# Attention scores as two rounded products over 128 stacked rows, and y and values in paired calls, in a decoder layer on one core

## The chip, the cores and the metric

One Trainium2 chip, one of its cores. The metric is the device time of one execution of the whole kernel in microseconds (us). TensorE (PE, with PEld for its weight loads), VectorE (DVE), ScalarE (ACT) and GpSimd (POOL) each run a list of instructions of their own in order and wait for each other by semaphores; SyncE (SP) issues the DMAs.

## The reference

A decoder layer over 64 sequences of 256 tokens and 256 features: a state-space mixer, cross attention of the 256 tokens to 376 rows (120 of a context, 256 of the sequence itself), and a gated "twist" block with three cycles. Each block is added to its input and normalised. The part that the change touches first is the attention, 8 heads of 64 features:

```python
q = ln @ Wq
kv = jnp.concatenate([xn, ln], axis=-2) @ Wkv
k, v = jnp.split(kv, 2, axis=-1)
q, k, v = (to_heads(q) * scale, to_heads(k), to_heads(v))
sim = jnp.einsum('bhid,bhjd->bhij', q, k)
attn = jax.nn.softmax(sim, axis=-1)
out = jnp.einsum('bhij,bhjd->bhid', attn, v)
```

The other part is the product of a chunk of the mixer, `y`, of the decay matrix `Lm` (tokens by tokens, per head) with `xdt` (tokens by 64 features, per head).

## The kernel before

The kernel is written by hand as one list of calls for each engine, and these lists set the order; there is no scheduler. A call such as `scores(s, c, i)` belongs to sequence `s`, and each engine has its own function of that name or of the step that follows it. In the steady loop (`for p in range(2, NSEQ - 1)`) three sequences are in work at once: `m` in the mixer, `a = m - 1` in the attention, `f = m - 2` in the twist block. Each pass of the loop finishes one sequence of work on each engine.

A result of TensorE goes to one of 8 PSUM banks. The scores take banks 1 to 3 in turn, the attention's other products 4 and 5, the mixer's 6 and 7, and the twist block bank 0. A bank is taken again when the engine that reads it has signalled.

Three kinds of TensorE product occur. Most are float32 products with both operands on 128 rows (or 120); the profile has two records for each such matmul. The projections use operands split into a rounded part `_hi` and a rest `_lo` in the rounded format float32r, and `product3` (L253) adds hi by hi, lo by hi and hi by lo; these have one record each. And three places use a part of the array: `scores` (L428) has 64 rows per head and puts the two heads of a pair on rows 0 to 63 and 64 to 127, plain float32; `values` (L452) and `y_pair` (L325) have 64 output columns per head.

Around the scores: `q_pair` and `k_tile` project q and k for two heads at a time into PSUM. ScalarE copies them to SBUF (`q_out` L952 into `q_sb`, one copy of 512 columns for each half of the heads; `k_out` L960 into `kT`, one copy of 376 columns for each of 4 head pairs). TensorE then makes 16 score tiles of 128 x 376 for each sequence, in 8 calls of two. VectorE takes the row maximum of each (`top`, L1638), ScalarE the exponential (`exp`, L979), TensorE turns the result (`turn`, L438), and ScalarE and VectorE copy the turned tiles out in equal parts (L989, L1657). `values` multiplies them with V, one call for each of 4 head pairs, and `divide` (L1666) applies the softmax sums.

VectorE has further the convolution taps (L1442), the splits into hi and lo (L1631, L1687, L1438), the three cycles of the twist block (`cycle`: L1716 to L1729), the sum and the norms of the output (`out_sum` L1738 to L1741, `out_norm` L1430) and `x1_raw`, `x1_norm` (L1576, L1595). GpSimd masks and scales the decay matrix (`masked` L2126, `times_g` L2139), forms `g`, and raises variances to the power -1/2 for all norms (L2117, L2175).

## Time and profile before

| | |
|---|---|
| median of 3 runs | 3862.34 us (3861.68 to 3863.0) |
| span of the profiled execution | 3861.4 us |
| PE busy | 3783.3 us, 98% |
| DVE busy | 3286.2 us, 85% |
| ACT busy | 3237.9 us, 84% |
| POOL busy | 1748.5 us, 45% |
| DMA, share of 16 engines | 18% |

The profiled execution lies inside the spread of the timed runs, 0.9 us below their median. A busy time is the union of an engine's instructions as recorded; on TensorE the ends of matmuls are modelled and consecutive records overlap, so there the distance from one start to the next says more than a duration.

### The profile page before, as it was taken

The numbers are of one execution on the slowest core, as the hardware profiler recorded it, in microseconds if no ns is written. First come the engines' busy times: TensorE is split into PE (matmuls) and PEld (weight loads), VectorE is DVE, ScalarE is ACT, GpSimd is POOL, SyncE is SP. The second block draws the span as 40 slices with busy tenths as digits, with TensorE's granted clock in tenths as the row PEclk, the third lists the DMA queues.
The fourth block names the chain that finished last, engine by engine and source line by source line (L and its number), as shares of the span: only waits on it lengthen the run. The fifth ranks groups of instructions, "written<-read, shape, count | busy, mean of one in ns | idle before, by whom it ended". The sixth has DMA issues, their size and how long they took to land.

```text
span 3861.4 us, 77375 instructions
## 1 busy us (share of the span) xinstructions
PE 3783.3 (98%) x25728; PEld 3000.9 (78%) x25728; DVE 3286.2 (85%) x8098; ACT 3237.9 (84%) x7812; POOL 1748.5 (45%) x3084
## 2 busy tenths in 40 slices
PE   6999999999999999999999999999999999999997
PEld 5777877877877878778778778777787787787775
DVE  7888888888888888888888888888888888888874
ACT  5788888888888888888888888888888888888885
POOL 3444445354454444453544544534535445445442
PEclk8999999999999999999999999999999999999998
DMA  3111112111211111121111111111211211111110
GB/s 97 54 47 59 55 45 61 54 42 58 58 45 55 48 59 54 45 61 53 43 57 59 45 55 50 56 55 45 61 55 42 61 55 45 55 54 53 55 38 17
DMA packets 312350, 203.14 MB, mean 53 GB/s; under 512 B 55056, under 2 KB 310928, under 8 KB 311952
## 3 DMA queue, kind: packets, MB, share of 16 engines
q1 hardware_dynamic: 311952, 198.20, 17.5%
q8 instruction: 206, 3.38, 0.4%
q14 instruction: 192, 1.57, 0.1%
HBM read 180.17 MB, written 17.96 MB: 51 GB/s over the span
## 4 chain that ended last, share of the span: by engine, by line
PE 59%; ACT 16%; DVE 15%; issue 4%; POOL 4%; DMA 1%; SPq 0%; DVEq 0%; POOLq 0%
PE psum L253 20%; PE psum L428 8%; PE psum L338 6%; PE psum L463 5%; PE psum L438 5%; PE psum L452 4%; PE psum L325 4%; ACT prob L979 3%; ACT h L1021 2%; ACT L979 2%; ACT L1021 2%; PE psum L497 2%; ACT xc L891 2%; POOL rs_mix L2175 2%; DVE nmax L1638 1%
## 5 line engine op out<-in xcount | busy, mean ns | idle before, releaser
L979 ACT ACTIVATE prob<-psum,nmax 128x376 f32<-128x376 f32 x1024 | 585.2, 575 | 49.5 <-DVE nmax L1638 46.2
L1638 DVE TENSOR_REDUCE nmax<-psum 128x1 f32<-128x376 f32 x1024 | 541.5, 540 | 14.4 <-PE psum L428 11.0
L2139 POOL TENSOR_TENSOR Lm<-Lm,G 128x384 f32<-128x384 f32 x512 | 506.1, 1012 | 92.8 <-DVE out_sb L1741 68.4
L438 PE MATMUL psum<-ident,prob 128*128 128x128 f32 (+1 forms) x3072 | 480.5, 276 | 2.1 <-ACT probT L989 1.1
L1442 DVE SCALAR_TENSOR_TENSOR u<-psum,par,u 128x253 f32<-128x253 f32 (+5 forms) x960 | 449.1, 479 | 28.1 <-ACT u L882 1.7
L428 PE MATMUL psum<-kT,q_sb 64*128 64x376 f32 x2048 | 467.7, 528 | 0.2 <-ACT prob L979 0.2
L438 PEld LDWEIGHTS psum<-ident,prob 128*128 128x128 f32 (+1 forms) x3072 | 363.0, 141 | 73.9 <-issue 45.0
L989 ACT ACTIVATE probT<-psum 128x384 f32<-128x384 f32 x512 | 252.7, 494 | 182.7 <-PE psum L438 182.5
L2126 POOL TENSOR_SCALAR_AFFINE_SELECT Lm<-Lm 128x256 f32<-128x256 f32 x512 | 205.7, 435 | 411.6 <-DMA Lm<-cum_row 411.6
L253 PE MATMUL psum<-x_hi,w_in_hi 128*128 128x256 f32 (+1 forms) x1152 | 360.9, 313 | 22.5 <-DVE w_in_lo L1764 9.3
L452 PE MATMUL psum<-probT,V 128*64 128x256 f32 (+1 forms) x3072 | 375.0, 385 | 0.3 <-ACT probT L989 0.3
L253 PE MATMUL psum<-x_hi,w_in_lo 128*128 128x256 f32 (+1 forms) x1152 | 326.0, 283 | 0.0
L253 PE MATMUL psum<-x_lo,w_in_hi 128*128 128x256 f32 (+1 forms) x1152 | 325.4, 283 | 0.0
L452 PEld LDWEIGHTS psum<-probT,V 128*64 128x64 f32 (+1 forms) x3072 | 202.4, 136 | 134.5 <-ACT probT L989 33.0
L1657 DVE COPY probT<-psum 128x384 f32<-128x384 f32 x512 | 279.9, 547 | 31.4 <-PE psum L438 27.2
L2194 POOL TENSOR_TENSOR h_a<-h_a,cpl 128x512 f32<-128x512 f32 x64 | 82.0, 1281 | 492.3 <-DVE h_pre L1724 492.3
L915 ACT ACTIVATE Lm<-Lm,ncum 128x256 f32<-128x256 f32 x512 | 262.8, 513 | 0.7 <-DVE ncum L1533 0.7
L463 PE MATMUL psum<-wo_sb,oT 128*128 128x256 f32 x1024 | 248.3, 386 | 0.7 <-DVE oT L1666 0.7
L979 ACT ACT_TABLE_LOAD x189 | 242.5, 1283 | 3.3
L338 PE MATMUL psum<-w_out_sb,g 128*128 128x256 f32 x1024 | 237.8, 386 | 0.0
L253 PEld LDWEIGHTS psum<-x_hi,w_in_hi 128*128 128x128 f32 (+1 forms) x1152 | 215.0, 187 | 28.4 <-issue 12.8
L463 PEld LDWEIGHTS psum<-wo_sb,oT 128*128 128x128 f32 x1024 | 189.4, 190 | 58.7 <-issue 32.9
(222 smaller groups left out, 11157.9 us busy)
## 6 DMA issues: line engine op xcount, KB each, us to landing
Lm<-cum_row SPq DMA_DIRECT2D x64, 1024.0 KB, 5.2
Lm<-cum_row SPq DMA_DIRECT2D x64, 512.0 KB, 6.5
invT<-inv_row SPq DMA_DIRECT2D x256, 128.0 KB, 3.0
xT_sb<-in_xT SPq DMA_DIRECT2D x64, 256.0 KB, 3.1
x_sb<-in_x SPq DMA_DIRECT2D x64, 256.0 KB, 3.3
result<-out_sb SPq DMA_DIRECT2D x64, 256.0 KB, 2.2
inv_row<-inv_t SPq DMA_DIRECT2D x512, 1.0 KB
ctx_sb<-in_ctx SPq DMA_DIRECT2D x64, 120.0 KB, 2.7
```

Source lines behind the costliest of these rows:

```text
L253: t = mm(dst, a, b, start=n == 1, stop=n == 3 * KT)
L338: t = mm(banks[b][:, i * D:(i + 1) * D], g[:, c, i * P:(i + 1) * P], w_out_sb[:, c, :], start=c == 0, stop=c == CT - 1)
L428: mm(banks[b][:, 0:NK], q_sb[r, c, i * P:(i + 1) * P], kT[r, c, :], start=True, stop=True).then_inc(p_sc, 1)
L438: t = tr(banks[b][0:m, j * P:(j + 1) * P], prob[:, r, j0:j0 + m], ident[:, :])
L452: t = mm(banks[b][k * HD:(k + 1) * HD, 0:L], V[0:m, j, h * HD:(h + 1) * HD], probT[0:m, (8 * s + h) % HP, j, :], start=j == 0, stop=j == l ...
L463: t = mm(banks[b][:, 0:D], oT[:, c, i * P:(i + 1) * P], wo_sb[:, c, :], start=c == 0, stop=c == CT - 1)
L915: act(Lm[:, h, 0:L], Lm[:, h, 0:L], ACT.Exp, bias=ncum[:, 0, h:h + 1])
L979: act(prob[:, r, :], b[:, 0:NK], ACT.Exp, bias=nmax[:, n:n + 1], accum_out=psum_row[:, n:n + 1]).then_inc(a_exp, 1)
L1442: stt(u[0:rows, c, d:L], src[:, 0:L - d], prm("conv_w", 4 * c + 3 - d, slice(0, rows)), u[0:rows, c, d:L], ALU.mult, ALU.add).then_inc(don ...
L1638: e.tensor_reduce(nmax[:, n:n + 1], banks[bank_of["sc", s, n]][:, 0:NK], AX.X, ALU.max, negate=True).then_inc(d_max, 1)
L1657: cp(probT[:, (8 * s + 2 * c + k) % HP, :, i * P:(i + 1) * P], b[:, 0:len(JT) * P].rearrange("p (j t) -> p j t", j=len(JT))).then_inc(d_tn, 1)
L2139: t = tt(Lm[:, h, :], Lm[:, h, :], G[:, :], ALU.mult)
```

## The change

**Scores.** `q_sb` and `kT` are replaced by stacks of 128 rows per head in float32r. `k_st` holds for each head the rounded k on the head's own 64 rows and the rest (k minus rounded k) on the other 64. `q_st` has two parts per head, rounded q and its rest, and each stands on both row halves. `scores` makes for each tile two products of 376 columns in full-array mode, rounded q over both halves of `k_st` and the rest of q over both halves, into one PSUM bank; together these are all four terms.

**Who fills the stacks.** ScalarE writes the rounded parts in two copies where there was one, because the two heads of a pair go to different rows of different tiles. VectorE gets `q_low` and `k_low`, which subtract the rounded part from PSUM (4 instructions of 64 x 512 and 8 of 64 x 376 for each sequence). GpSimd gets `spread_q`, which copies both parts of q to the other row half: 4 copies of 64 x 1024 for each sequence, each group led by a `memset` of one column and waits for its own semaphore. The scores wait for `k_low` (`d_k`) and the copies (`l_fence`) where they waited for ScalarE. The banks of q and k are freed by VectorE.

**Pairs.** `y_pair` and `values` become calls of two head pairs that share one bank; the copies out of it wait for both.

**Banks.** All but the scores take turns on five banks, the scores on three.

**Order.** All call lists are rewritten. The loop starts at another point of the same pipeline (the twist block of `m - 3` at its top is that of `m - 2` after `out_proj(m)`).

**Small parts.** `x_sb` has one buffer instead of two; the weight loads stand in another order; the instruction lists hold 504 loads of an activation table on ScalarE, where they held 445.

```diff
@@ tiles
-        q_sb, kT = sb("q_sb", [P, CT, L]), sb("kT", [P, CT, NK])
+        q_st = sb("q_st", [P, 2, H, L], F32R)
+        k_st = sb("k_st", [P, H, NK], F32R)
+        fence = sb("fence", [P, 1])
@@ TensorE
             def scores(s, c, i):
-                n = 2 * (TT * c + i)
-                pe.wait_ge(a_q, 2 * s + c // 2 + 1)
-                pe.wait_ge(a_k, 4 * s + c + 1)
+                pe.wait_ge(d_k, 4 * s + c + 1)
+                pe.wait_ge(l_fence, 6 * s + 3 * (c // 2) + 3)
                 for k in range(2):
-                    b = bank_of["sc", s, n + k] = take(ring_s)
-                    r = slice(k * HD, (k + 1) * HD)
-                    mm(banks[b][:, 0:NK], q_sb[r, c, i * P:(i + 1) * P], kT[r, c, :], start=True, stop=True).then_inc(p_sc, 1)
-                    freed[b] = [(a_exp, 16 * s + n + k + 1)]
+                    h, n = 2 * c + k, 2 * (TT * c + i) + k
+                    b = bank_of["sc", s, n] = take(ring_s)
+                    for part in range(2):
+                        t = mm(banks[b][:, 0:NK], q_st[:, part, h, i * P:(i + 1) * P], k_st[:, h, :], start=part == 0, stop=part == 1)
+                    t.then_inc(p_sc, 1)
+                    freed[b] = [(a_exp, 16 * s + n + 1)]
@@ ScalarE
-                act(q_sb[:, 2 * j:2 * j + 2, :], b[:, :].rearrange("p (c t) -> p c t", c=2), ACT.Copy).then_inc(a_q, 1)
+                for k in range(2):
+                    r = slice(k * HD, (k + 1) * HD)
+                    t = act(q_st[r, 0, 4 * j + k:4 * j + 4:2, :], b[r, :, :], ACT.Copy)
+                t.then_inc(a_q, 1)
...
-                act(kT[:, c, :], b[:, 0:NK], ACT.Copy).then_inc(a_k, 1)
+                for k in range(2):
+                    r = slice(k * HD, (k + 1) * HD)
+                    t = act(k_st[r, 2 * c + k, :], b[r, 0:NK], ACT.Copy)
+                t.then_inc(a_k, 1)
@@ VectorE
+            def q_low(s, j):
+                if not live(s):
+                    return
+                b = banks[bank_of["q", s, j]].rearrange("p (c t) -> p c t", c=2)
+                ve.wait_ge(a_q, 2 * s + j + 1)
+                for k in range(2):
+                    r, hs = slice(k * HD, (k + 1) * HD), slice(4 * j + k, 4 * j + 4, 2)
+                    t = tt(q_st[r, 1, hs, :], b[r, :, :], q_st[r, 0, hs, :].bitcast(F32), ALU.subtract)
+                t.then_inc(d_q, 1)
+            def k_low(s, c):
+                if not live(s):
+                    return
+                b = banks[bank_of["k", s, c]]
+                ve.wait_ge(a_k, 4 * s + c + 1)
+                for k in range(2):
+                    r, other = slice(k * HD, (k + 1) * HD), slice((1 - k) * HD, (2 - k) * HD)
+                    t = tt(k_st[other, 2 * c + k, :], b[r, 0:NK], k_st[r, 2 * c + k, :].bitcast(F32), ALU.subtract)
+                t.then_inc(d_k, 1)
@@ GpSimd
+            def spread_q(s, j):
+                if not live(s):
+                    return
+                po.wait_ge(d_q, 2 * s + j + 1)
+                n = 6 * s + 3 * j
+                e.memset(fence[:, :], 0.0).then_inc(l_fence, 1)
+                po.wait_ge(l_fence, n + 1)
+                for k in range(2):
+                    r, other = slice(k * HD, (k + 1) * HD), slice((1 - k) * HD, (2 - k) * HD)
+                    hs = slice(4 * j + k, 4 * j + 4, 2)
+                    t = e.tensor_copy(q_st[other, :, hs, :], q_st[r, :, hs, :]).then_inc(l_fence, 1)
+                    po.wait_ge(l_fence, n + 2 + k)
@@ TensorE, pairs (values likewise)
-            def y_pair(s, q):
+            def y_half(s, d):
...
+                for q in (2 * d, 2 * d + 1):
+                    pe.wait_ge(l_Lm, 4 * s + q + 1)
+                    o = q % 2 * L
...
+                freed[b] = [(d_yD, 4 * s + 2 * d + 2)]
```

Three places show how the instructions move. TensorE in the steady loop, around one call of the scores. Before, between the projection of z (`w_in`) and the turned tiles, the four records of a head pair are two matmuls of 64 rows:

```order
L253 MATMUL psum<-x_lo,w_in_hi 128x256
L428 MATMUL psum<-kT,q_sb 128x376 x2
L253 MATMUL psum<-wkv_hi,kv_hi 120x512
...
L463 MATMUL psum<-wo_sb,oT 128x256 x4
L438 MATMUL psum<-ident,prob 120x128
L438 MATMUL psum<-ident,prob 128x128 x2
L428 MATMUL psum<-kT,q_sb 128x376 x2
L325 MATMUL psum<-Lm,xdt 64x256 x2
```

And now:

```order
L468 MATMUL psum<-wo_sb,oT 128x256 x4
L430 MATMUL psum<-k_st,q_st 128x376 x4
L254 MATMUL psum<-kv_hi,wkv_hi 128x376
...
L254 MATMUL psum<-wkv_hi,kv_lo 128x512
L313 MATMUL psum<-ident,xc 128x128 x4
L430 MATMUL psum<-k_st,q_st 128x376 x4
L441 MATMUL psum<-ident,prob 120x128
```

A call of the scores is now four products of the full array between others of the same kind or transposes.

VectorE from the constant of the twist block on (`c_cyc`, `base`), where its first cycle stands. Before, the cycle is followed by the taps of the convolution:

```order
L1631 TENSOR_TENSOR kv_lo<-kv,kv_hi 128x2x256
L1638 TENSOR_REDUCE nmax<-psum 128x1
L1706 SCALAR_TENSOR_TENSOR c_cyc<-tg,gf_gain,c_base 128x1
L1716 TENSOR_SCALAR cpl<-cpl,tf_gain,c_cyc 128x256
L1721 TENSOR_TENSOR h_pre<-h_b,cpl 128x512
L1724 TENSOR_TENSOR h_pre<-h_pre,h_a 128x512
L1442 SCALAR_TENSOR_TENSOR u<-psum,par,u 128x255
```

And now the rests of q and k stand before and behind it:

```order
L1745 SCALAR_TENSOR_TENSOR c_cyc<-tg,gf_gain,c_base 128x1
L1666 TENSOR_TENSOR q_st<-psum,q_st 64x2x256 x2
L1755 TENSOR_SCALAR cpl<-cpl,tf_gain,c_cyc 128x256
L1760 TENSOR_TENSOR h_pre<-h_b,cpl 128x512
L1763 TENSOR_TENSOR h_pre<-h_pre,h_a 128x512
L1676 TENSOR_TENSOR k_st<-psum,k_st 64x376 x2
L1705 TENSOR_TENSOR oT<-oT,invT 128x512
L1696 COPY probT<-psum 128x3x128 x2
L1676 TENSOR_TENSOR k_st<-psum,k_st 64x376 x2
```

Six new instructions stand within these nine rows; nothing was taken off VectorE's list anywhere.

GpSimd between the norm of the mixer and the factors of the output. Before:

```order
L2175 TENSOR_TENSOR rs_mix<-ve_mix,minus_half 128x4
L2194 TENSOR_TENSOR h_a<-h_a,cpl 128x512
L2196 TENSOR_TENSOR h_b<-h_b,h_a 128x512
L2126 AFFINE_SELECT Lm<-Lm 128x2x128 x6
L2209 TENSOR_TENSOR cd<-c_col 128x2
```

And now:

```order
L2260 TENSOR_TENSOR rs_mix<-ve_mix,minus_half 128x4
L2187 TENSOR_SCALAR ve_ctx<-mv_ctx 120x1
L2189 TENSOR_TENSOR rs_ctx<-ve_ctx,minus_half 120x1
L2187 TENSOR_SCALAR ve_ffn<-mv_ffn 128x1
L2189 TENSOR_TENSOR rs_ffn<-ve_ffn,minus_half 128x1
L2228 MEMSET fence 128x1
L2233 COPY q_st<-q_st 64x2x2x256 x2
L2279 TENSOR_TENSOR h_a<-h_a,cpl 128x512
L2281 TENSOR_TENSOR h_b<-h_b,h_a 128x512
L2198 AFFINE_SELECT Lm<-Lm 128x2x128 x6
```

The copies of q stand ahead of the twist's products and of the masks.

## Rows read from the trace of the kernel before

**Rows 1.** One stretch of the steady loop: busy time (instructions) of each engine, clock, DMA.
```profile
core 0: us, PE busy (x) PEld busy (x) DVE busy (x) ACT busy (x) POOL busy (x), PEclk, DMA share, GB/s
1000.00:3500.00 2500.00, 2487.82 (x17043) 1976.59 (x17043) 2168.11 (x5343) 2142.40 (x5180) 1157.54 (x2046) 1.00 0.18 53
```

**Rows 2.** ACT's copy of G, one per sequence: ns min/median/max, first and last start (us).
```profile
L908 ACT ACTIVATE G<-psum x44: 480/490/492, 954.2 to 3489.0; 128x384 f32<-128x384 f32 x44
```

**Rows 3.** PE in order of time: start, us, engine, line, tiles, count.
```profile
1901.35 0.28 PE L253 MATMUL psum<-x_hi,w_in_lo 128*128 128x256 f32 x1
1901.47 0.28 PE L253 MATMUL psum<-x_lo,w_in_hi 128*128 128x256 f32 x1
1901.67 0.90 PE L428 MATMUL psum<-kT,q_sb 64*128 64x376 f32 x4
1902.51 0.49 PE L253 MATMUL psum<-wkv_hi,kv_hi 128*120 128x512 f32 x1
1902.83 0.39 PE L253 MATMUL psum<-wkv_lo,kv_hi 128*120 128x512 f32 x1
...
1903.99 1.89 PE L463 MATMUL psum<-wo_sb,oT 128*128 128x256 f32 x8
1905.72 0.49 PE L438 MATMUL psum<-ident,prob 128*120 128x128 f32 x3
```

**Rows 4.** The same view, a k tile: the last five of its six rounded products.
```profile
1909.19 0.33 PE L253 MATMUL psum<-kv_hi,wkv_lo 128*128 128x376 f32 x1
...
1909.87 0.34 PE L253 MATMUL psum<-kv_lo,wkv_hi 128*128 128x376 f32 x1
1910.05 0.49 PE L438 MATMUL psum<-ident,prob 128*120 128x128 f32 x3
```

**Rows 5.** DVE in order of time, operations near to the new ones in shape.
```profile
1903.81 1.00 DVE L1638 TENSOR_REDUCE nmax<-psum 128x1 f32<-128x376 f32 x2
...
1934.53 0.69 DVE L1631 TENSOR_TENSOR kv_lo<-kv,kv_hi 128x512 fp32r<-128x512 f32 x1
1935.14 0.54 DVE L1638 TENSOR_REDUCE nmax<-psum 128x1 f32<-128x376 f32 x1
```

**Rows 6.** What DVE waited for from 1000 to 3500: us, times, longest; ten rows.
```profile
DVE cpl L1716 <- ACT cpl L1033: 50.7, 43, 1.2
DVE out_sb L1738 <- POOL of_minus L2226: 50.2, 43, 1.2
DVE x_pre L1576 <- PE psum L338: 40.4, 42, 1.0
DVE x_n L1595 <- POOL rs_mix L2175: 34.1, 42, 0.8
DVE out_sb L1430 <- POOL rs_ffn L2117: 19.7, 43, 0.5
...
DVE oT L1666 <- DMA invT<-inv_row: 1.8, 6, 0.5
```

**Rows 7.** DVE and POOL in order of time at the two norms of one output.
```profile
1020.17 0.41 DVE L1430 TENSOR_SCALAR out_sb<-out_sb,mv_ffn,rs_ffn 128x256 f32<-128x256 f32 x1
...
1020.98 2.00 POOL L2139 TENSOR_TENSOR Lm<-Lm,G 128x384 f32<-128x384 f32 x2
1021.04 1.08 DVE L1430 TENSOR_SCALAR out_sb<-out_sb,mv_ffn,rs_ffn 128x256 f32<-128x256 f32 x1 [0.46 <-POOL rs_ffn L2117]
```

**Rows 8.** Groups by line, shapes apart: count, busy us, mean ns, idle before.
```profile
L960 ACT ACTIVATE kT<-psum 128x376 f32<-128x376 f32 x256 | 123.2, 481 | 2.4 <-PE psum L253 2.4
L952 ACT ACTIVATE q_sb<-psum 128x512 f32<-128x512 f32 x128 | 75.1, 587 | 3.6 <-PE psum L253 3.4
L1021 ACT ACT_TABLE_LOAD x125 | 160.4, 1283 | 2.2
L2231 POOL CAST cw_hi<-h_a 128x512 fp32r<-128x512 f32 x1 | 0.6, 612 | 0.0
L2194 POOL TENSOR_TENSOR h_a<-h_a,cpl 128x512 f32<-128x512 f32 x64 | 82.0, 1281 | 492.3 <-DVE h_pre L1724 492.3
```

More of the change, by code:

```diff
@@ new lines, in _ @@
+            in_x(last, 1)
+            scores(last - 2, 3, 1)
+            layer(last - 3, 0, 2)
+            q_pair(last - 1, 0)
+            twisted(last - 3)
+            turn(last - 2, 11)
+            layer(last - 3, 0, 3)
+            k_tile(last - 1, 0)
+            turn(last - 2, 12)
+            turn(last - 2, 13)
+            k_tile(last - 1, 1)
+            scores(last - 1, 0, 0)
+            layer(last - 3, 1, 1)
+            turn(last - 2, 14)
+            turn(last - 2, 15)
+            layer(last - 3, 1, 2)
@@ L1908, in _ @@
[L1908 to L1927 removed]
+            x1_norm(1)
```

1459 lines of the change are left out of this document (753 added, 706 removed).

## Prediction

> **What bounds the kernel now.** I read the loop first, then each engine against it. From 1000 to 3500 us TensorE is busy 2487.82 of 2500 us, at a granted clock of 1.00 [rows 1]: it hardly ever waits, so it is the bound, and the time is the number of sequences times the length of a pass. ScalarE's copy of G comes once for each sequence, and between the first and the last of 44 lie 43 passes in 3489.0 - 954.2 = 2534.8 us [rows 2], so **a pass is 58.95 us**. In that pass TensorE works 58.95 x 2487.82 / 2500 = 58.66 us, VectorE 51.1, ScalarE 50.5, GpSimd 27.3 [rows 1]. VectorE is second, and the distance is what matters here, because the change takes work from TensorE and gives VectorE more.
>
> How much of VectorE's idle time is really free? It is idle 58.95 - 51.12 = 7.8 us of a pass. The view of its waits in that stretch has ten rows, which sum to 247.7 us in 390 waits [rows 6], that is 5.8 us of a pass in 9 waits. The other 2.0 us are gaps between its own dependent instructions, which stay. Against that, back-to-back instructions overlap: two maxima take 1.00 us and one 0.54 [rows 5], so an instruction before a wait gives up 0.08 us, 0.7 us a pass. **VectorE thus needs 58.95 - 5.8 - 0.7 = 52.4 us a pass** and has 6.5 us of room.
>
> **TensorE: the scores.** A call of the scores before starts 0.20 us after the last 256-column rounded product, where the next such product comes after 0.12 (1901.35 to 1901.47): 0.08 for going to 64 rows. Its four records take 1902.51 - 1901.67 = 0.84 us. The 512-column product behind it takes 0.32 until the next, where two of 256 columns take 0.24: another 0.08. Sum 1.00 us [rows 3]. After, it is four rounded products of 376 columns in full-array mode. Such products start (1910.05 - 1909.19) / 5 = 0.172 us apart [rows 4], so 0.69 us; coming from plain float32 work may cost another 0 to 0.1, and I take 0.04. Saved: 0.27 us, 8 times a pass, 2.2 us.
>
> **TensorE: the pairs.** The half-width products (y and values) stood in five places of a pass and stand in three, since two calls of y are now side by side and values come in twos. Each place saved is worth the two changes of shape of [rows 3], 0.16 us: together 0.3 us, bounds 0 and 0.5. The matmuls are the same. TensorE then needs 58.66 - 2.2 - 0.3, **about 56.1 us a pass**. Over 64 sequences that would be 165 us, if TensorE stayed the bound.
>
> A rule of the Trainium skill speaks against this edit. The row pairs start together and run side by side: a plain float32 record of 256 columns takes (1905.72 - 1903.99) / 8 = 0.216 us [rows 3], 0.318 scaled to 376, so four in a row would take 1.27 us and a perfect pair 0.64, while 0.84 was measured. TensorEngine Tiling (Array Packing), section Theoretical Speedup, promises up to 2x for a dimension of at most 64. By that the pair would cost 0.64 and the full-array form, 0.69, would lose; by the row it is 0.84. The row decides.
>
> **VectorE: the rests.** It gets 8 subtractions of 64 x 376 and 4 of 64 x 512 for each sequence, and loses nothing. The number of rows plays no part that I can see, so I go by columns: maxima of 376 columns start 1.00 - 0.54 = 0.46 us apart, and a two-input operation of 512 columns is followed by the next after 1935.14 - 1934.53 = 0.61 [rows 5]. 8 x 0.46 + 4 x 0.61 = **6.1 us a pass**. Bounds: without overlap 8 x 0.54 + 4 x 0.69 = 7.1; below, nothing, since each is a full pass over its columns. VectorE then needs 52.4 + 6.1 = **58.5 us a pass, more than TensorE's 56.1**. The room of 6.5 us is used up to 0.4 us. The bound moves to VectorE, and TensorE's 2.6 us turn into waiting.
>
> **ScalarE.** A second copy for each: 4 x 0.48 + 2 x 0.59 = 3.1 us a pass [rows 8], and 59 more table loads in the list, 59 x 1.283 / 64 = 1.2 us. 50.5 + 4.3 = 54.8 us. It lies beside VectorE's 58.5 and is hidden; without that cover it would cost the whole 4.3.
>
> **GpSimd.** Four copies of 64 x 1024. A converting copy of 512 columns takes 0.612 us, a two-input product 1.281 [rows 8]; twice these are 1.2 and 2.6, and a copy is nearer to the first. 4.9 us a pass, bound 10.3, beside 27.3: there is room. But the copies are queued ahead of the twist's products, the masks and `times_g`. Behind them stand VectorE's second cycle and TensorE's y. And the scores now wait for a chain of a ScalarE copy, two VectorE subtractions and two GpSimd copies, 1.0 + 1.2 + 2.5 = 4.7 us, where it was one copy of 0.59. In the new list two k tiles or the second projection and some turned tiles stand between `q_pair` and the scores that need it, several us of TensorE work; I cost the chain at nothing in the loop. Single-buffered x, five shared banks and the new order of weight loads: nothing; DMA is at 18% [rows 1].
>
> **The sum.** A pass lasts VectorE's 58.5 us and what it still waits for. The least is what the bound engine waits now: 2500 - 2487.82 = 12.2 us in 42 passes, 0.3 us. The most I expect in an order made anew is half of today's 5.8, 2.9 us. The other engines have room (TensorE 2.4, ScalarE 3.7 us), but three engines are now within 7% of each other, where the second was 11% off; and the waits of [rows 6] come from chains through ScalarE and GpSimd that still exist. I take 0.9, nearer to the low end. Pass: 59.4 us, 0.45 more than before. 63 passes x 0.45 = +28 us on the execution's own 3861.4, which is 0.9 below the median of the runs: 3861.4 + 28 + 0.9 = **3890 us**. The ends I leave as they are: the last sequence gains 8 x 0.27 us on TensorE and pays the longer chain once or twice, within 10 us either way.
>
> **Rivals.**
> - **VectorE packed as tightly as TensorE was.** Waits of 0.3, and the blocked norm gone. One of the two output norms takes 1.08 us instead of 0.41 when a GpSimd product has just started [rows 7], 0.67 a pass; in another order it may not meet one. 58.5 - 0.67 + 0.3 = 58.1 up to 58.8 us a pass, 3809 to 3853 us: faster than before. It decides as soon as VectorE waits less than 0.4 us a pass. For it: TensorE achieved 0.3 with the second engine 11% behind. Against: the same room is not there.
> - **TensorE stays the bound**, the subtractions cheaper than any row suggests: 56.1 + 0.3 = 56.4 us, -2.55 x 63 = -161, 3701 us. It needs VectorE to spend 4 us or less on 12 operations, 0.33 each, which is the rate of 256 columns and not of 376 or 512.
> - **GpSimd's copies hold up VectorE**, by blocking it or by delaying what is queued behind them. Each further meeting like [rows 7] costs up to 0.67 us; three a pass with waits of 0.9 give 58.5 + 2.0 + 0.9 = 61.4 us, +154, 4016 us. It decides from 1.2 us a pass on, where the time passes 3965. The Trainium skill has this as a rule: SBUF — State Buffer, section "SBUF: two separate sides", says that VectorE and GpSimd share one port pair that is held for a whole instruction, and the other is blocked. The trace agrees [rows 7].
>
> **How the numbers follow.** VectorE binds with some waiting, 3855 to 3965 us: 0.58, of which 0.12 lies within 0.2% of before (about what a measurement of this kernel can tell from no change), 3855 to 3870. Tight packing, below 3855: 0.26. TensorE bound: 0.04. GpSimd in the way, above 3965: 0.12. Faster 0.26 + 0.04 = 0.30, same 0.12, slower 0.46 + 0.12 = 0.58. The range goes from the tightest packing to 2.1 us of waiting, 3810 to 3965, and leaves out TensorE as the bound and the third rival, 0.16.
>
> **What would show it.** TensorE's busy time in the loop falls to 95 or 96% and it has waits that it had not; VectorE's rises to 97% or more. The four score products take 0.69 us from start to start of the next group. The groups of `k_st` and `q_st` on VectorE have means of 0.54 and 0.69 us, and a pass, by the copies of G, 59.4 us. The view of VectorE's waits shrinks from 5.8 to about 1 us a pass. It would be wrong if VectorE still waits 3 us or more while TensorE does too (a chain binds, not an engine), or if the subtractions from 64 rows to the other 64 have another price than their columns.

## The result

| | before | after |
|---|---|---|
| median | 3862.67 us (3861.68 to 3864.47) | **4296.02 us** (4295.66 to 4297.52) |
| span of the profiled execution | 3861.4 us | 4293.9 us |
| ratio, 95% interval | | **1.1121 (1.1105 to 1.1137)** |

The changed kernel is 11.2% slower. That is the sign to which I gave the larger chance, but far outside the range of 3810 to 3965. The steady loop alone is read as before: the first fence is the stretch of [rows 1], the second the copy of G of [rows 2], and the columns are theirs.

```profile
1000.00:3500.00 2500.00, 2226.59 (x15244) 1909.86 (x15243) 2354.94 (x5224) 2093.43 (x4886) 1264.72 (x2043) 0.98 0.16 47
```

```profile
L913 ACT ACTIVATE G<-psum x39: 478/481/483, 991.0 to 3498.4; 128x384 f32<-128x384 f32 x39
```

A pass is (3498.4 - 991.0) / 38 = **65.98 us**, 7.03 more than 58.95. TensorE is busy for 89% of it, VectorE for 94%: 2354.94 / 2500 x 65.98 = 62.15 us, where it was 51.12. So VectorE idles 3.8 us a pass instead of 7.8, and 11.0 - 4.0 is the 7.0. The page of the profile says the same by the chain of work that ended last: by engine before, then by engine and by line in the changed kernel.

```profile
PE 59%; ACT 16%; DVE 15%; issue 4%; POOL 4%; DMA 1%; SPq 0%; DVEq 0%; POOLq 0%
```

```profile
DVE 73%; issue 12%; ACT 6%; PE 4%; POOL 3%; DVEq 0%; DMA 0%; SPq 0%; ACTq 0%; POOLq 0%
DVE nmax L1657 11%; DVE u L1461 10%; DVE probT L1696 5%; DVE k_st L1676 4%; DVE oT L1705 3%; DVE q_st L1666 2%; DVE xc L1575 2%; DVE h_pre L1760 2%; POOL rs_mix L2260 2%; DVE xdt L1565 2%; DVE x L1449 2%; ACT q_st L959 2%; DVE dt_e L1480 2%; DVE xc L1514 1%; DVE kv_hi L1648 1%
```

What TensorE now waits for in that stretch (us in total, times, longest), where before it waited some 12 us in all:

```profile
PE psum L430 <- DVE k_st L1676: 97.6, 38, 2.6
PE psum L254 <- DVE x_lo L1457: 58.4, 37, 1.6
PE psum L534 <- ACT g L1070: 39.5, 38, 1.1
PE psum L341 <- POOL g L2221: 35.1, 38, 0.9
```

The scores wait for the rests of k, once a pass and 2.6 us long. The next fences show what VectorE itself spends: one group of the kernel before, then groups of the changed kernel in the same stretch (count, busy us, mean ns, idle before), then the group of the GpSimd copies over the whole execution.

```profile
L1721 DVE TENSOR_TENSOR h_pre<-h_b,cpl 128x512 f32<-128x512 f32 x42 | 29.1, 693 | 1.4
```

```profile
L1676 DVE TENSOR_TENSOR k_st<-psum,k_st 64x376 fp32r<-64x376 f32 x304 | 166.4, 547 | 6.7
L1666 DVE TENSOR_TENSOR q_st<-psum,q_st 64x512 fp32r<-64x512 f32 x152 | 104.7, 689 | 29.9 <-ACT q_st L959 28.4
L1705 DVE TENSOR_TENSOR oT<-oT,invT 128x512 f32<-128x512 f32 x76 | 88.2, 1160 | 1.2
L1760 DVE TENSOR_TENSOR h_pre<-h_b,cpl 128x512 f32<-128x512 f32 x38 | 53.4, 1406 | 1.3
L1763 DVE TENSOR_TENSOR h_pre<-h_pre,h_a 128x512 f32<-128x512 f32 x38 | 50.9, 1341 | 4.0
L1449 DVE TENSOR_SCALAR x<-x,mv_att,rs_att 128x256 f32<-128x256 f32 x76 | 50.5, 704 | 1.2
...
L1480 DVE SCALAR_TENSOR_TENSOR dt_e<-dt_a 8x256 f32<-8x256 f32 x38 | 41.0, 1078 | 1.2
```

```profile
L2233 POOL CAST q_st<-q_st 64x1024 fp32r<-64x1024 f32 x256 | 295.3, 1154 | 16.8
```

Two things stand there. The new subtractions have the means I gave (0.547 and 0.689 us) but don't overlap: together they take 7.15 us a pass, where I had 6.1 and an upper bound of 7.1. And VectorE operations that took 692 ns (`h_pre`) or 415 ns (`dt_e`) before now take 1.3 to 1.4 us and 1.08 us. In order of time, VectorE and then GpSimd at one such place:

```profile
2023.88 1.39 DVE L1666 TENSOR_TENSOR q_st<-psum,q_st 64x512 fp32r<-64x512 f32 x2
2025.30 0.41 DVE L1755 TENSOR_SCALAR cpl<-cpl,tf_gain,c_cyc 128x256 f32<-128x256 f32 x1
2025.75 1.41 DVE L1760 TENSOR_TENSOR h_pre<-h_b,cpl 128x512 f32<-128x512 f32 x1
2027.26 1.34 DVE L1763 TENSOR_TENSOR h_pre<-h_pre,h_a 128x512 f32<-128x512 f32 x1
2028.63 1.11 DVE L1676 TENSOR_TENSOR k_st<-psum,k_st 64x376 fp32r<-64x376 f32 x2
```

```profile
2025.33 0.10 POOL L2228 MEMSET fence<- 128x1 f32 x1 [7.37 <-DVE q_st L1666]
2025.50 2.56 POOL L2233 CAST q_st<-q_st 64x1024 fp32r<-64x1024 f32 x2
```

The two copies begin 1.62 us after `q_low` began on VectorE, because `q_low` releases them. The two `h_pre` products that follow `q_low` in VectorE's list meet them in every pass (1404 to 1410 ns and 1339 to 1343 ns over all 38 of the stretch), and each takes twice its time. Counted over all lines that grew, VectorE operations are 4.9 us a pass longer than before. Of this I put 2.2 down to the copies (one `divide` of two +0.83, `h_pre` +0.72 and +0.65), and the rest to GpSimd products that meet others in the new lists (`dt_e` +0.66, the norm of x +0.60, the splits `kv_lo`, `kv_hi`, `x2T_lo` +0.42, +0.36, +0.41, `xc` +0.21 and smaller ones). One meeting of before, the norm of [rows 7], is gone: -0.71.

### The profile page after: what moved, and what is told of

Same layout as the page of the kernel before. It is cut to its first block, busy times and chain, and to the rows that moved or that the text cites. A ratio compares the mean times of both kernels' runs of the same rounds, so it can differ in the third digit from the quotient of the medians.

```text
span 4293.9 us, 79467 instructions
## 1 busy us (share of the span) xinstructions
PE 3780.5 (88%) x25728; PEld 3239.6 (75%) x25728; DVE 3992.2 (93%) x8869; ACT 3534.1 (82%) x8255; POOL 2140.7 (50%) x3468
## 4 chain that ended last, share of the span: by engine, by line
DVE 73%; issue 12%; ACT 6%; PE 4%; POOL 3%; DVEq 0%; DMA 0%; SPq 0%; ACTq 0%; POOLq 0%
DVE nmax L1657 11%; DVE u L1461 10%; DVE probT L1696 5%; DVE k_st L1676 4%; DVE oT L1705 3%; DVE q_st L1666 2%; DVE xc L1575 2%; DVE h_pre L1760 2%; POOL rs_mix L2260 2%; DVE xdt L1565 2%; DVE x L1449 2%; ACT q_st L959 2%; DVE dt_e L1480 2%; DVE xc L1514 1%; DVE kv_hi L1648 1%
## 5 line engine op out<-in xcount | busy, mean ns | idle before, releaser
L430 PE MATMUL psum<-k_st,q_st 128*128 128x376 f32 x2048 | 496.4, 365 | 159.7 <-DVE k_st L1676 158.8
L430 PEld LDWEIGHTS psum<-k_st,q_st 128*128 128x128 f32 x2048 | 355.7, 194 | 191.8 <-DVE k_st L1676 178.0
L1461 DVE SCALAR_TENSOR_TENSOR u<-psum,par,u 128x255 f32<-128x255 f32 (+5 forms) x960 | 448.9, 478 | 24.0 <-ACT u L887 0.9
L254 PE MATMUL psum<-x_hi,w_in_hi 128*128 128x256 f32 (+1 forms) x1152 | 345.9, 300 | 107.1 <-DVE x_lo L1457 94.6
L457 PE MATMUL psum<-probT,V 128*64 128x256 f32 (+1 forms) x3072 | 360.5, 383 | 0.0
L2233 POOL CAST q_st<-q_st 64x1024 fp32r<-64x1024 f32 x256 | 295.3, 1154 | 16.8
L970 ACT ACTIVATE k_st<-psum 64x376 fp32r<-64x376 f32 x512 | 244.1, 477 | 65.8 <-PE psum L254 61.3
L2221 POOL TENSOR_TENSOR g<-xc,gate 128x256 f32<-128x256 f32 x256 | 205.2, 823 | 185.5 <-DVE xc L1575 185.5
L1676 DVE TENSOR_TENSOR k_st<-psum,k_st 64x376 fp32r<-64x376 f32 x512 | 280.2, 547 | 13.3 <-ACT k_st L970 2.0
L504 PE MATMUL psum<-h,cw_sb 128*128 128x256 f32 x768 | 241.8, 444 | 32.6 <-DVE k_st L1676 22.9
```

Source lines behind the costliest of these rows:

```text
L254: t = mm(dst, a, b, start=n == 1, stop=n == 3 * KT)
L430: t = mm(banks[b][:, 0:NK], q_st[:, part, h, i * P:(i + 1) * P], k_st[:, h, :], start=part == 0, stop=part == 1)
L457: t = mm(banks[b][k * HD:(k + 1) * HD, o:o + L], V[0:m, j, h * HD:(h + 1) * HD], probT[0:m, (8 * s + h) % HP, j, :], start=j == 0, stop=j ...
L970: t = act(k_st[r, 2 * c + k, :], b[r, 0:NK], ACT.Copy)
L1461: stt(u[0:rows, c, d:L], src[:, 0:L - d], prm("conv_w", 4 * c + 3 - d, slice(0, rows)), u[0:rows, c, d:L], ALU.mult, ALU.add).then_inc(don ...
L1676: t = tt(k_st[other, 2 * c + k, :], b[r, 0:NK], k_st[r, 2 * c + k, :].bitcast(F32), ALU.subtract)
```

## The experiments

All times are medians; a ratio is to the kernel before in runs on the same chip. "VectorE's time" is its busy time of 1000 to 3500 us times the pass over 2500, and "idle" is the rest of the pass. A pass is read from the copies of G each time. At the start there were two theories. Theory A: VectorE is the bound, and what counts is its work and what GpSimd adds to it. Theory B: the redrawn lists and longer chains bind. Each expectation says what A and B mean for its run. All runs together, the time in us and the rest in us a pass:

| kernel | time | pass | VectorE's time | idle | TensorE's time |
|---|---|---|---|---|---|
| before | 3863 | 58.95 | 51.1 | 7.8 | 58.7 |
| one rounded product a score block | 3834 | 58.52 | 51.2 | 7.3 | 56.1 |
| new score form alone | 3841 | 58.64 | 51.2 | 7.4 | 57.1 |
| paired calls alone | 3972 | 60.43 | 51.6 | 8.9 | 58.7 |
| 4 subtractions, place 1 | 4071 | 62.27 | 55.3 | 6.9 | 59.4 |
| 4 subtractions, place 2 | 3987 | 60.91 | 54.0 | 6.9 | 60.0 |
| one product and 4 subtractions, place 2 | 3961 | 60.53 | 53.9 | 6.6 | 56.9 |
| 4 GpSimd copies | 3989 | 61.00 | 53.4 | 7.6 | 59.2 |
| 4 GpSimd copies elsewhere | 3989 | 60.90 | 53.4 | 7.5 | 59.7 |
| 13 subtractions | 4231 | 64.81 | 59.3 | 5.5 | 60.9 |
| 13 subtractions and 4 copies | 4347 | 66.58 | 61.2 | 5.4 | 61.2 |
| new lists, old scores | 4033 | 61.76 | 53.4 | 8.4 | 58.9 |
| the same, inverse first | 3988 | 60.92 | 53.3 | 7.6 | 58.6 |
| after, no rests, no copies | 4048 | 61.97 | 55.3 | 6.7 | 57.8 |
| after, copies of 4 columns | 4172 | 63.94 | 60.0 | 3.9 | 58.0 |
| after, rests of k of one column | 4211 | 64.61 | 60.0 | 4.6 | 57.9 |
| after, same rows | 4273 | 65.60 | 61.7 | 3.9 | 58.6 |
| after | 4296 | 65.98 | 62.2 | 3.8 | 58.8 |
| after, inverse first | 4302 | 66.05 | 62.2 | 3.9 | 58.8 |
| after, copies by DMA | 4307 | 66.04 | 60.1 | 6.0 | 59.0 |

### In the changed kernel: parts of the load taken away

**The copies on one column of each head.** In `spread_q`:

```
-t = e.tensor_copy(q_st[other, :, hs, :], q_st[r, :, hs, :])
+t = e.tensor_copy(q_st[other, :, hs, 0:1], q_st[r, :, hs, 0:1])
```

> The changed kernel, GpSimd's four copies of q per sequence cut from 1024 columns to 4 (one per head and part); all waits stay, the scores are made with mostly empty second row halves of q. Theory A (VectorE is the bound, and GpSimd instructions block it): the three long operations that meet a copy now (divide +0.83 us, the two products of the first cycle +0.71 and +0.65) go back to 0.69 us, 2.2 us of a pass of 66.0; 63 passes give -139 us, 4155 us, pass 63.8. Theory B (the new order and its longer chains bind, not VectorE's load): the chain to the scores gets shorter by 2.3 us but VectorE's list is what it was: 4260 to 4296 us.

4172.27 us, ratio 1.0795 (1.0777 to 1.0813). 124 us less (141 expected), 2.04 a pass, and VectorE's time falls by 2.2. The groups of `h_pre`, which took 1406 and 1341 ns, in this run:

```profile
L1760 DVE TENSOR_TENSOR h_pre<-h_b,cpl 128x512 f32<-128x512 f32 x39 | 27.0, 693 | 1.3
L1763 DVE TENSOR_TENSOR h_pre<-h_pre,h_a 128x512 f32<-128x512 f32 x39 | 27.0, 692 | 4.1
```

Theory A holds here: the copies cost what they block. The chain to the scores got shorter in the same edit, but VectorE's idle time stayed at 3.9 us a pass, so the whole gain is VectorE's time.

**The rests of k on one column.**

```
-t = tt(k_st[other, 2 * c + k, :], b[r, 0:NK], k_st[r, 2 * c + k, :].bitcast(F32), ALU.subtract)
+t = tt(k_st[other, 2 * c + k, 0:1], b[r, 0:1], k_st[r, 2 * c + k, 0:1].bitcast(F32), ALU.subtract)
```

> The changed kernel, the eight subtractions for the rest of k per sequence cut from 376 columns to 1 (the rest of k is left out of the scores, all waits stay). Theory A: each falls from 0.57 us start to start to about 0.15, 3.3 us of a pass: -210 us, 4085 us. Theory B: the chain to the scores is shorter by about 0.8 us per k tile, at most -50 us.

4210.97 us, ratio 1.0895 (1.0879 to 1.0912): 85 us less, not 211. `k_st` itself went from 4.39 to 1.25 us a pass, but VectorE's time fell by 2.2 only. `divide` now meets both copies, with a mean of 1555 ns where it was 1160, and the norm of x has 1038 where it was 704; one meeting (`dt_e`) is gone:

```profile
L1705 DVE TENSOR_TENSOR oT<-oT,invT 128x512 f32<-128x512 f32 x78 | 121.3, 1555 | 1.5 <-DMA invT<-inv_row 0.3
L1449 DVE TENSOR_SCALAR x<-x,mv_att,rs_att 128x256 f32<-128x256 f32 x76 | 75.9, 1038 | 1.3
L1480 DVE SCALAR_TENSOR_TENSOR dt_e<-dt_a 8x256 f32<-8x256 f32 x38 | 15.8, 415 | 1.2
```

Work taken from VectorE shifts all that follows against GpSimd, and other pairs meet. Theory A's sum by work alone does not hold for such an edit.

**The copies by DMA.** `spread_q` moves from GpSimd to SyncE's queue (`e.dma_start(q_st[other, part, hs, :], q_st[r, part, hs, :])`, two for each part and half of the heads), and the scores wait for its semaphore.

> The changed kernel, the copies of q to the other row half made by DMAs from SBUF to SBUF on SP's queue instead of GpSimd; result complete. Theory A: no GpSimd copy is left to block VectorE, so as with the copies cut, 63 x 2.2 = -139 us, 4155 us, if the DMA (3 us from issue to landing, against 2.3 us for two copies) does not make the scores late; masks and factors on GpSimd come earlier, which can make other meetings. Theory B: no gain, 4290 to 4340 us, since the chain is longer.

4306.89 us, ratio 1.114 (1.1124 to 1.1157). The blocking by the copies is gone (VectorE's time falls by 2.1), but nothing is won: VectorE's idle time rises by the same 2.1, and TensorE's longest wait is now the one of the scores for these DMAs.

```profile
PE psum L429 <- DMA q_st<-q_st: 134.0, 38, 5.0
```

That is 3.5 us a pass, where the scores waited 2.6 for the rests of k. The chain of 4.7 us that I had costed at nothing is not free once it is longer. How much of the wait is the transfer and how much its place in SyncE's queue was not separated.

**Rests of k with both heads on the same rows.** In `k_low`:

```
-r, other = slice(k * HD, (k + 1) * HD), slice((1 - k) * HD, (2 - k) * HD)
+r, other = slice(0, HD), slice(HD, P)
```

> The changed kernel with both subtractions of a k tile reading rows 0 to 63 and writing rows 64 to 127 (half of the k rests are wrong so), all else as it is. If consecutive VectorE operations overlap only on the same rows, the two then start 0.46 to 0.50 us apart instead of 0.57, 4 x 0.1 us a pass, and up to twice that where a maximum is the neighbour: 4245 to 4275 us. If the rows play no part: 4290 to 4303 us.

4272.78 us, ratio 1.1057 (1.1041 to 1.1074), 23 us less, at the upper end of the first range. A pair of subtractions in this kernel, and then one in the changed kernel:

```profile
2017.46 1.00 DVE L1676 TENSOR_TENSOR k_st<-psum,k_st 64x376 fp32r<-64x376 f32 x2
```

```profile
2031.65 1.11 DVE L1676 TENSOR_TENSOR k_st<-psum,k_st 64x376 fp32r<-64x376 f32 x2
```

With the same rows two take 1.00 us, as two maxima do in [rows 5]; on different rows 1.11, each at its full length with a small gap. The four saved overlaps are 0.4 us a pass, and the pass is 0.39 shorter.

**Rests and copies both gone** (the two edits above and the same for the rests of q).

> The changed kernel with both parts of the new load nearly gone: the 8 + 4 subtractions and the GpSimd copies work on one column a row (the k and q rests and the other half of q are so left out); lists, score form, banks and ScalarE's copies as changed. Theory A (VectorE's time sets the pass, part by part): 66.0 less 2.1 (copies) less about 5.2 (subtractions) is 58.7 us a pass, 3835 to 3870 us. Theory B (below VectorE's time stands a chain of the redrawn lists, 61.8 us a pass with float32 scores, at best 1.6 less with the new form): 60.2 to 61.8 us a pass, 3930 to 4035 us.

4047.8 us, ratio 1.0472 (1.0457 to 1.0488). This is theory B's case, slightly above its upper end: with most of the new load gone the new lists and score form still take 61.97 us a pass, 3.0 more than before. So of the 7.0 us the load taken away is 4.0, and **3.0 stay without it**. Not all load is gone: the 12 subtractions of one column still take 0.16 us each, 1.9 us a pass. And `divide` here waits for the DMA of the inverse sums again (23.3 us in the stretch), the trip that the next runs look at.

### The redrawn lists

**Old float32 scores in the new lists.** `q_sb`, `kT` and `scores` are those of before; `q_low`, `k_low` and `spread_q` return at once; lists, pairs and banks are the changed ones.

> The changed kernel with the scores of before: plain float32 pairs of 64 rows, one ScalarE copy per q half and k tile, no subtractions on VectorE, no copies on GpSimd; order, pairs and banks as changed. Theory A: VectorE loses 7.2 us of subtractions and 2.2 of blocking, 66.0 - 9.4 = 56.6 us a pass, below TensorE's 58.66 - 0.3; TensorE binds at 58.6 to 59.5 us, 3840 to 3900 us. Theory B (the order is at fault): most of the loss stays, over 4050 us.

4032.73 us, ratio 1.0436 (1.042 to 1.0452). This lies between the two theories, and no engine is full: TensorE 95%, VectorE 86%. The chain of waits at one place of the loop, in order of time (start, us, what):

```profile
2012.18 0.69 DVE dc L1528
2012.88 1.30 DMA cum_row<-dc
...
2015.30 0.87 SPq L2470
...
2016.89 4.84 DMA inv_row<-inv_t
2021.75 0.58 SPq L2480
2022.37 2.96 DMA invT<-inv_row
```

The inverse sums of the softmax (`inv_t`) go out to memory and back, 4.84 + 2.96 us, and are issued only behind the cumulative sums of another sequence: the loop has `spread_cum(m)` ahead of `keep_inv(f, 0)`. That is one line to move.

**The same with the inverse first.**

```
-spread_cum(m)
 keep_inv(f, 0)
+spread_cum(m)
 spread_inv(f, 0)
```

> The redrawn lists with the old float32 scores (as in the run of the new order), and on the DMA queue of SyncE the first half of the inverse sums is written out ahead of the cumulative sums instead of behind them. Theory A (no queue but the engines matters): 4020 to 4045 us as without it. Theory B (in the redrawn lists the chain cumulative sums, then inverse sums out and in by DMA, then VectorE's division binds the pass, as the chain of waits says, 4.84 + 2.96 us of it): 1 to 2 us a pass less, 3900 to 3980 us.

3988.2 us, ratio 1.032 (1.0305 to 1.0336), 44.5 us less, or 0.84 a pass, a little under the 1 to 2 of theory B. The queue on SyncE was in the chain. What its head waited for, first with the new list, then with the line moved:

```profile
SPq L2455 <- DVE dc L1528: 1414.0, 41, 34.9
```

```profile
SPq L2470 <- DVE inv_t L1681: 1254.7, 82, 27.0
...
SPq L2455 <- DVE dc L1528: 266.1, 41, 6.5
```

**And in the changed kernel.** The same move in it.

> The changed kernel whole, with the first half of the inverse sums written out ahead of the cumulative sums on SyncE's DMA queue instead of behind them. With float32 scores that had given 44 us back. If VectorE's own time hides that trip in the changed kernel (it waits only 1.65 us a pass): 4285 to 4300 us. If the trip is in its chain too: 4250 us or less.

4302.19 us, ratio 1.1129 (1.111 to 1.1147): nothing gained. In the changed kernel VectorE has no wait for the inverse sums in the stretch, so the trip is hidden behind its own work. A stall of the new lists is worth 44 us in one kernel and nothing in the other.

**Paired calls alone, in the old lists.** y and values in calls of two head pairs in one bank, a pair where its second half stood.

> The kernel before with y and values in paired calls of 512 columns in one bank (a pair stands where its second half stood), all else as it was: float32 scores, ring of banks, the other calls of the lists in their places. Theory A (the pairs save TensorE two changes of shape for each pair of calls, and their coarser banks cost nothing): 59 us a pass less 0.3, 3840 to 3862 us. Theory B (the pairs hold a bank longer and let what needs their first half wait, which is a part of what the float32 scores in the new order had lost): 3890 us or more.

3971.66 us, ratio 1.0278 (1.0263 to 1.0294). I had taken 0.3 us a pass off for the pairs. TensorE's time is unchanged (58.7), and the pass is 1.5 us longer: VectorE's waits grow (the twist's coefficient `cpl`, 76.3 us in the stretch where [rows 6] has 50.7; `xc` behind the paired y, 42.9 where it was 14.0), and TensorE waits 1.1 us a pass for the twist's `g`. How much of this belongs to my placing of the pairs and not to the pairs I can't tell from this run.

### In the kernel before: parts of the load added

**VectorE's load.** 13 subtractions whose results are not used, in `top`:

```
+if n % 5 or n == 15:
+    ve.wait_ge(d_max, 16 * s + n - 1)
+    lo, hi = (slice(0, HD), slice(HD, P))[::1 if n % 2 else -1]
+    tt(rest[hi, :], banks[bank_of["sc", s, n]][lo, 0:NK], wkv_hi[lo, 0, 0:NK].bitcast(F32), ALU.subtract)
 e.tensor_reduce(nmax[:, n:n + 1], ...)
```

The tile `rest` for the results takes memory, and with it comes the smaller DMA scratch of the changed kernel (`dynamic_dma_scratch_size=256`). All runs that add a tile to the kernel before have it, and no run separates it.

> The kernel before, with its lists, banks and float32 scores as they are, and 13 added subtractions for each sequence on VectorE, of 64 x 376 from a score bank to the other 64 rows, one ahead of a maximum; their results are not used. Only VectorE's work is raised, by about the 7.15 us a pass that the rests cost in the changed kernel (13 x 0.55 = 7.1). Theory A (VectorE's own work, and what GpSimd adds to it, sets the pass): VectorE then needs 52.4 + 7.1 = 59.5 us, plus 0.3 to 1.5 us of waits, pass 59.8 to 61.0, 3915 to 3990 us. Theory B (the chains of the redrawn lists set it, VectorE's work is not what counts): TensorE stays the bound, 3862 to 3890 us.

4230.57 us, ratio 1.095 (1.0934 to 1.0966). This is far over what I expected from the "room". VectorE's time rose by 8.1 us a pass and its idle time fell by only 2.3.

**GpSimd's load.** Four copies of 64 x 1024, two behind `mix`, two behind the third mask.

> The kernel before with four added copies of 64 x 1024 for each sequence on GpSimd (two after the weights of the mix, two after the third mask), whose results are not used. Theory A: they make some VectorE instructions longer, by up to 1.15 us each, at most 4.6 us a pass; VectorE has 6.5 us of room, so TensorE stays the bound and the time stays within 20 us of 3863. Theory B (GpSimd's longer queue delays what stands behind it, and the chain through it binds): 3900 us or more.

3988.51 us, ratio 1.0327 (1.031 to 1.0344). That is 2 us a pass, with a cause in plain sight, GpSimd first, then VectorE:

```profile
2048.27 1.03 POOL L2188 TENSOR_TENSOR rs_mix<-ve_mix,minus_half 128x4 f32<-128x4 f32 x1
2049.25 0.10 POOL L2157 MEMSET fence<- 128x1 f32 x1
2049.42 2.13 POOL L2161 CAST spare<-spare 64x1024 fp32r<-64x1024 f32 x2
```

```profile
2049.34 2.36 DVE L1597 TENSOR_SCALAR x_n<-x_pre,mv_mix,rs_mix 128x256 f32<-128x256 f32 x2 [0.81 <-POOL rs_mix L2188]
```

`x_n` has waited for `rs_mix`, starts, and GpSimd starts its copies next to it. TensorE waited 1.0 us a pass for `x_n`. I took that meeting for the cause.

**The copies elsewhere**, behind the third mask and behind the factors.

> The run with four added GpSimd copies a sequence in the old kernel, with the copies elsewhere in GpSimd's queue: two behind the third mask and two behind the factors, none behind the weights of the mix, where they made VectorE's two x_n operations 2.36 us long instead of 0.7 and TensorE waited 1.0 us for them in each pass. Theory A (the price of a GpSimd instruction is that of the VectorE instruction it meets and of who waits for that one): back to within 25 us of 3863. Theory B (it is the amount of GpSimd work, or of blocked time, wherever it stands): 3950 us or more as before the move.

3989.24 us, ratio 1.0327 (1.031 to 1.0344), the same time. `x_n` is back at 410 ns, and now the sums of the output meet the copies (415 and 362 ns before):

```profile
L1743 DVE SCALAR_TENSOR_TENSOR out_sb<-x,of_minus,out_sb 128x128 f32<-128x128 f32 x82 | 68.0, 829 | 0.0
L1742 DVE SCALAR_TENSOR_TENSOR out_sb<-x,of_tw,out_sb 128x128 f32<-128x128 f32 x82 | 56.6, 690 | 2.9
```

VectorE's time is 2.2 us longer in both, and so is the pass, by 2.0. My refinement (the price is that of the one operation met) fell; the amount of blocked time stayed, wherever it was.

**Both loads.**

> The kernel before with both loads, the 13 subtractions on VectorE and the four copies on GpSimd; lists, banks and scores stay. Theory A: VectorE needs 59.5 us, the copies add 1 to 3 us to it, waits 0.3 to 1.5: pass 60.8 to 64, 3980 to 4180 us, and more than the two single loads together cost. Theory B: no more than the two single loads together.

4346.76 us, ratio 1.1245 (1.1228 to 1.1262): 483 us, and the two single loads are 366.7 + 124.7 = 491. They add up; theory A had them cost more together than apart. This is more than the changed kernel takes. So the redrawn lists carry such a load better than the old ones do with it at these places: 62.2 us of VectorE's time in a pass of 66.0, where the old lists need 66.6 for 61.2.

**Four subtractions, at two places.** The condition becomes `n % 4 == 3`, or `n % 4 == 1`.

> The kernel before with four added subtractions of 64 x 376 a sequence on VectorE, ahead of the maxima 3, 7, 11 and 15 (2.2 us a pass of VectorE time). If VectorE's room of 6.5 us is real: 3862 to 3875 us. If its idle time is no room, because the waits belong to chains that pass through it: 1.5 to 2.2 us a pass more, 3955 to 4000 us.

> As the run with four added subtractions, with them ahead of the maxima 1, 5, 9 and 13. If the amount of VectorE time decides: within 15 us of that run. If the place decides (whose chain they lengthen): over 25 us away from it.

4071.08 us, ratio 1.0533 (1.0518 to 1.0549), and 3986.53 us, ratio 1.0313 (1.0298 to 1.0328). 2.2 us of VectorE work a pass cost 3.3 us at one place and 2.0 at the other, so the place counts as well. With what GpSimd added by new meetings VectorE's time rose by 4.2 and 2.8, and in both its idle time gave only 0.9. The first has a new meeting, with a GpSimd product on 512 columns, VectorE and then GpSimd:

```profile
2021.56 1.52 DVE L1462 SCALAR_TENSOR_TENSOR dt_e<-dt_a 8x256 f32<-8x256 f32 x1
```

```profile
2021.50 1.30 POOL L2160 TENSOR_TENSOR gate<-gate 128x512 f32<-128x512 f32 x1 [5.32 <-ACT gate L923]
```

`dt_e` has 0.41 us before and 1.52 here, and TensorE waits 1.3 us for the taps `u` behind it. Neither place is free. The room of 6.5 us was not there for 2.2. One thing these runs leave open: every added subtraction stands ahead of a maximum, on the way from a score tile to its exponential, and no place off that way was tried. The GpSimd copies, which lengthened other operations (`x_n`, `out_sb`), cost 2.0 us for 2.2 all the same.

### In the kernel before: TensorE relieved

**The new score form alone.** `q_sb` and `kT` are float32r, and a score block is two full-array products; no rests, no copies.

```
-mm(banks[b][:, 0:NK], q_sb[r, c, i * P:(i + 1) * P], kT[r, c, :], start=True, stop=True)
+for part in range(2):
+    t = mm(banks[b][:, 0:NK], q_sb[:, c, i * P:(i + 1) * P], kT[:, c, :], start=part == 0, stop=part == 1)
```

> The kernel before with the form of the scores alone: q and k tiles are written rounded, and each score block is two rounded full-array products of 376 columns over 128 rows instead of one of a float32 row pair. No rests, no copies, lists as before; the scores are not the reference's. My step for TensorE says 8 x 0.27 = 2.2 us a pass saved: if TensorE stays full, 56.8 to 57.5 us a pass, 3730 to 3775 us. Against it stands that TensorE's busy time in the changed kernel is 58.8 us a pass where 56.1 was worked out: if the form saves nothing, 3855 to 3870 us. In between, with TensorE now waiting for ScalarE or VectorE in the loop: the products are cheaper, but a chain takes part of it.

3841.25 us, ratio 0.9941 (0.9926 to 0.9956). On TensorE in order of time:

```profile
2005.00 0.28 PE L253 MATMUL psum<-x_lo,w_in_hi 128*128 128x256 f32 x1
2005.12 0.85 PE L428 MATMUL psum<-kT,q_sb 128*128 128x376 f32 x4
2005.80 0.39 PE L253 MATMUL psum<-wkv_hi,kv_hi 128*120 128x512 f32 x1
```

0.68 us from the four products to the next, where I had worked out 0.69; after plain float32 work it is some 0.8 (TensorE's time fell by 1.6 us a pass, not 2.2). And the pass fell by 0.3. The rest went into waits that TensorE had not had, 0.7 us a pass for `xc` of VectorE and 0.6 for `h` of ScalarE.

**One rounded product of 64 rows for each score block** (q and k rounded, their rests left out), in place of the float32 one.

> The kernel before with each score block as one rounded product of 64 rows instead of a float32 one (q and k are written rounded; their rests are left out), all else as it is. TensorE is relieved of 8 x (1.0 - about 0.35) = 5 us a pass or so, VectorE and ScalarE of nothing. Theory A (TensorE is the bound of the old lists, VectorE has 6.5 us of room): 54 to 56.5 us a pass, 3560 to 3710 us. Theory B (VectorE's chains stand just below it, so that little of it reaches the pass): 58.2 to 58.7 us a pass, 3815 to 3845 us.

> The same with the four added subtractions on VectorE ahead of the maxima 1, 5, 9 and 13, which cost the kernel before 2.0 us a pass. Theory A: with TensorE relieved and VectorE with room, within 30 us of the run without them. Theory B: the chains through VectorE are lengthened as before, 110 to 140 us more than that run.

3834.0 us, ratio 0.9919 (0.9904 to 0.9933), and 3960.99 us, ratio 1.0246 (1.0229 to 1.0264). TensorE is relieved still more, to 56.1 us (by 2.6, where I expected about 5), and waits 2.5; VectorE idles 7.3 us, and the pass is 58.52. So **something other than TensorE's own work held the loop at 58.5 us**, 0.4 us behind it. By the chain of this run it is no single engine; TensorE's share, 59% before, is half of that:

```profile
PE 30%; ACT 24%; DVE 19%; POOL 12%; issue 9%; DMA 2%; SPq 0%; DVEq 0%; POOLq 0%
```

With TensorE out of the way the four subtractions cost 127 us, as they had cost 120 beside it. What TensorE waits for in the first:

```profile
PE psum L360 <- DVE xc L1556: 42.0, 43, 1.0
PE psum L497 <- ACT h L1021: 37.2, 84, 0.6
PE psum L253 <- DVE x_lo L1438: 17.5, 43, 1.3
```

This is the fastest kernel of the study, with less precise scores. Of the kernels that keep the rests of q and k, or float32, none is faster than the one before.

## Why the prediction was wrong

**The room of VectorE was the first step to fail.** I took all 5.8 us of its waits a pass for room, because TensorE was busy 99.5% of the time and so had to be what it waited for. They were waits in chains through several engines that were themselves almost as long as the pass: 58.5 us against 58.95, by the run with one product and its chain of waits. In the old lists four subtractions of 2.2 us cost 2.0 or 3.3 us of the pass, 2.2 us of blocking 2.0, and 13 subtractions 5.9. The waits of [rows 6] did not shrink to a fifth of themselves there, as I had it, but idle time went from 7.8 to 5.5 us. A busy share of 99.5% says that one engine is full, not that the others are free.

In the changed kernel the idle time does come out near my number, 3.8 us where I had 2.9. The step misjudged what the added work does in the old lists, and with it how near the edge the whole loop stood, but here it makes only 0.9 us of the 6.6 that the pass is off (65.98 against 59.4). The other 5.7 us are VectorE's time: 4.2 of blocking net of the old meeting, 1.05 of the subtractions, 0.4 of overlaps.

**GpSimd in the way was a rival at 0.12; in the sum it stood at nothing, and it is the largest single item of VectorE's time.** I priced a meeting at 0.67 us from [rows 7] and allowed three. The price was about right (the five longest cost 0.60 to 0.83 us, the others 0.2 to 0.4), the count was not: there are about ten a pass, 4.9 us, less 0.7 for the old one. The four copies account for 2.2 of it, which the run without them gives back as 124 us. The other 2.7 are read from the operations' lengths; no run took them away. The rule of the Trainium skill that I had cited (SBUF — State Buffer, section "SBUF: two separate sides") says that one pair of ports goes for a whole instruction either to GpSimd or to a VectorE operation that is in a two-port mode or has two SBUF inputs, the latter only against a GpSimd operation that reads SBUF. The trace agrees: `h_pre`, `divide` and `dt_e`, with both inputs in SBUF, were lengthened, and the subtractions from PSUM were not (542 to 553 ns for all 304 of 64 x 376), though GpSimd's product `h_a` runs beside one pair. I should have gone down the new lists with it, since the copies stand right behind `q_low` in time, and so do two operations of that kind. The mechanism had the evidence of one row and a rule, and I gave it 12%.

**The price of a subtraction** was worked out as 6.1 us a pass and measured as 7.15, at the upper bound of 7.1, which is 1.05 us of the miss. I wrote that the number of rows plays no part; which rows they are does. The run on the same rows shows 0.1 us a pair, 0.4 of the 1.05; for the rests of q this was not tried.

**The overlaps before waits** were 0.7 us a pass that I had taken off VectorE's need. VectorE's time in the changed kernel is 51.1 + 7.15 + 4.9 - 0.7 = 62.45 by its parts and 62.15 in the trace, so 0.3 of the 0.7 was real.

**The pairs and the lists at nothing.** -0.3 for the pairs was wrong in sign in the old lists (+1.5, with the caveat above), and the new lists with float32 scores need 61.8 us a pass before any new load is in them. That alone is 2.4 over the 59.4 that I forecast for the whole, with VectorE at only 53.4. So the order, which stood at nothing in the sum beyond 0.9 us of waiting, is a failed term of its own. One cause in the lists is shown, the inverse sums queued behind the cumulative sums on SyncE, 0.8 us. I had weighed the order by the calls next to the scores and not gone through SyncE's queue, because DMA is at 18% [rows 1]. The queue's share says nothing of a trip of 7.8 us that starts late. What else holds these lists at 60.9 is open.

**TensorE's scores** were right in kind: 0.68 us a call at best, and 1.6 us a pass of the 2.2. As TensorE was not alone at the limit, this was worth 0.3 us a pass.

**What was right.** In the changed kernel VectorE is the bound (94% busy, 73% of the chain), TensorE gets waits it had not and the longest is for the rests of k, the four copies and the subtractions have the lengths worked out (1.154 us for 1.2; 0.547 and 0.689), and the sign. I had named a VectorE share of 97%, and 94% came with 1.6 us of waits a pass, inside the bounds of 0.3 to 2.9. The size came out 15 times mine: 433 us for 28. The right sign owes little to the sum behind it: 0.45 us a pass was forecast, and terms that I had at nothing made most of the 7.0.

**How the 7.0 us divide.** New lists, pairs and banks with the old scores are +2.8; the new score form with ScalarE's split copies and what is left of the subtractions is +0.2; the rest of the subtractions and the copies are +4.0, and the copies alone, taken from the changed kernel, 2.0. These are differences between runs that each shift every engine, so they are a path from one kernel to the other and not shares that hold one by one: a like load costs +7.6 in the old lists.

## What to carry to other kernels

An engine that is 99.5% busy may have a chain through the others just behind it. So idle time of the second engine is room only after a run has shown it: take work off the first engine, or put a little on the second, and see what the pass does. When an edit adds a GpSimd instruction that a VectorE instruction releases, read which VectorE operations with only SBUF inputs come next in the list; here those were the ones that grew, `h_pre` to twice its time and `dt_e` to 2.6 times. And follow each round trip through a DMA queue whose order changes, however low the DMA share.
